# Selective scan, front work: VectorE empties the front's PSUM bank, input loads and silu move, three decay buffers

## What is computed

```python
xc   = silu(causal_conv(x_in, conv_w, 4 taps) + conv_b)          # [2, 2048, 512]
proj = xc @ xp_w.T                                               # 64 + 16 + 16 columns
dt, Bm, Cm = split(proj, [64, 80])
dt   = softplus(dt @ dt_w.T + dt_b)                              # [2, 2048, 512]
A    = -exp(A_log)                                               # [512, 16]
def step(h, (x_t, dt_t, B_t, C_t)):
    dA = exp(dt_t[:, :, None] * A)
    h  = dA * h + (dt_t * x_t)[:, :, None] * B_t[:, None, :]     # state: 512 channels x 16
    y  = einsum('bdn,bn->bd', h, C_t) + D * x_t
```

## Time and profile before

| | us |
|---|---|
| median of 3 runs | 4641.67 (4637.85 to 4651.1) |
| the profiled execution, its own time | 4628.16 |
| its span | 4626.6 |
| first scan to last scan | 251.8 to 2048 |
| mean length of a unit (15 from silu to silu) | 112.6 |
| busy in 256 to 1945: PE / DVE / ACT / POOL | 1303.4 / 1310.8 / 1481.8 / 1321.6 of 1689 |

### The profile page before, as it was taken

How to read it: one execution, slowest core, us unless ns; L and a number is a source line. 1 busy time by engine, 2 the same in 40 slices (tenths; PEclk the granted TensorE clock), 3 DMA queues, 4 the chain that set the end, 5 groups by cost and what they waited for, 6 DMA issues and landing times. The chain is left out here.

```text
span 4626.6 us, 69508 instructions
## 1 busy us (share of the span) xinstructions
PE 3557.3 (77%) x20742; PEld 2201.9 (48%) x20742; DVE 2819.4 (61%) x4258; ACT 2720.9 (59%) x4311; POOL 1749.6 (38%) x1132
## 2 busy tenths in 40 slices
PE   8477777777777777756775888888988885499990
PEld 4156666666666666645553222222222223366660
DVE  4267777777777777756675666666666665411105
ACT  3288888888888888864563455555555551011120
POOL 0067777777777777764342000000000002300006
PEclk9688889998888888877886899999999997699995
DMA  6443322233333333334545000100010103311115
GB/s 209 120 110 83 83 83 83 83 96 87 88 88 84 83 86 89 83 105 147 208 155 163 17 24 24 26 24 20 24 26 24 26 17 117 122 64 67 69 40 185
DMA packets 183442, 385.72 MB, mean 83 GB/s; under 512 B 21763, under 2 KB 96630, under 8 KB 168624
## 3 DMA queue, kind: packets, MB, share of 16 engines
q1 hardware_dynamic: 129360, 285.61, 21.3%
q10 hardware_dynamic: 39760, 51.81, 3.3%
q0 software_dynamic: 13968, 43.97, 2.8%
HBM read 272.97 MB, written 110.91 MB: 83 GB/s over the span
## 5 line engine op out<-in xcount | busy, mean ns | idle before, releaser
L730 DVE TENSOR_TENSOR_SCAN scan_hh<-scan_dA,scan_state,scan_bx 128x512 f32<-128x512 f32 x1024 | 1247.9, 1265 | 413.6 <-PE scan_bx L816 351.6
L507 POOL TENSOR_TENSOR scan_hC<-scan_hh,scan_cbc 128x1024 f32<-128x1024 f32 x512 | 1207.7, 2370 | 237.4 <-DVE scan_hh L730 137.2
L1464 DVE TENSOR_REDUCE attend_mx<-attend_s 128x1 f32<-128x512 f32 (+1 forms) x1360 | 781.5, 608 | 342.9 <-PE attend_s L1594 226.0
L816 PE MATMUL scan_bx<-kept_ident,scan_dBxT 128*128 128x128 f32 x4096 | 692.8, 297 | 104.6 <-DVE scan_hh L730 55.1
L573 ACT ACTIVATE scan_dBxT<-scan_dtxT,scan_bt 128x512 f32<-128x512 f32 x1028 | 655.8, 712 | 97.8 <-PE scan_bx L816 97.7
L826 PE MATMUL scan_acc<-kept_ident,scan_hC 128*128 128x128 f32 x4128 | 671.8, 292 | 43.1 <-ACT scan_uu L582 41.8
L568 ACT ACTIVATE scan_dA<-scan_dt,scan_an 128x512 f32<-128x512 f32 x1028 | 665.7, 714 | 50.6 <-DVE scan_hh L730 50.6
L816 PEld LDWEIGHTS scan_bx<-kept_ident,scan_dBxT 128*128 128x128 f32 x4096 | 525.5, 154 | 297.4 <-DVE scan_hh L730 154.2
L1558 ACT ACTIVATE attend_full<-attend_s 128x1024 f32<-128x1024 f32 x384 | 392.0, 1025 | 332.1 <-PE attend_s L1621 328.1
L1594 PE MATMUL attend_s<-attend_kt,attend_qt 96*128 96x512 bf16 (+1 forms) x1360 | 481.4, 372 | 130.9 <-DVE attend_mx L1464 73.3
L826 PEld LDWEIGHTS scan_acc<-kept_ident,scan_hC 128*128 128x128 f32 x4128 | 538.8, 153 | 47.2 <-ACT scan_uu L582 45.5
(11 more groups left out here) (219 smaller groups left out, 4502.3 us busy)
## 6 DMA issues: line engine op xcount, KB each, us to landing
scan_xs<-scratch_xin SPq DMA_DIRECT2D x288, 256.0 KB, 7.7
scan_cbc<-scratch_crows SPq DMA_DIRECT2D x64, 1024.0 KB, 5.0
scratch_qk<-mix_heads ACTq DMA_DIRECT2D x64, 384.0 KB, 10.0
scratch_y<-scan_uu ACTq DMA_DIRECT2D x17, 1024.0 KB, 4.2
attend_qt<-scratch_qk SPq DMA_DIRECT2D x34, 384.0 KB, 3.7
attend_kt<-scratch_qk SPq DMA_DIRECT2D x34, 384.0 KB, 4.5
mix_yf<-scratch_y SPq DMA_DIRECT2D x10, 1024.0 KB, 8.3
mix_yb<-scratch_y SPq DMA_DIRECT2D x10, 1024.0 KB, 12.0
```

Of the source, the lines that this page charges most:

```text
L507: pool.tensor_tensor(hC[n % 2][:, ms, :], h[:, ms, :], rows.unsqueeze(1).broadcast_to([P, 2, C]), ALU.mult).then_inc(hc_ok, 1)
L730: dve.tensor_tensor_scan(hh[n % 2][:, m, r], dA[n % 2][:, m, r], bx[bank(j)][:, r], state[:, d, n, m:m + 1], ALU.mult, ALU.add).then_inc(h ...
L816: last = pe.transpose(bx[bank(j)][:, t * P:(t + 1) * P], dBxT[turned_slot(n)][:, t, m * P:(m + 1) * P], k["ident"][:, :])
L1464: dve.tensor_reduce(mx[:, t, c:c + 1], s1[v % 2][:, 0:w], AX_X, ALU.max).then_inc(s1_read, 1)
```

## The change

- `conv_out` and `turned_out` move from ACT to DVE: an add of the bias (tensor_scalar, bank to SBUF) and a plain copy (bank to SBUF). In DVE's order each stands right behind the scan at whose j PE wrote the piece.
- conv of unit f + 2 is at j = 29, 33, 38, 43 (was 30, 36, 41, 58). All four blocks are ahead of turned dt*x, which stays at 49, 51, 53, 55.
- `silu` of unit f + 2 is in ACT's `tail(12)` of unit f, where `silu` of unit f + 1 was in `tail(0)`. Ahead of the first unit, ACT now runs silu twice.
- SP issues conv blocks 2 and 3 ahead of the last C rows (steps 12 to 15).
- dA has three buffers, in the order of dBxT's (`turned_slot`): n mod 3, but 1 for n = 15. `decay` waits by `decay_free`: three scans-of-a-step back in the middle of a unit, two for n = 15 and n = 1.

```diff
-        dA = [s.sb(f"dA{i}", [P, DT, C]) for i in range(2)]
+        dA = [s.sb(f"dA{i}", [P, DT, C]) for i in range(3)]
...
-        FR_PROJ, FR_BT, FR_DT, FR_NEXT, FR_TURN, FR_LAST, FR_ALL = 0, 1, 2, 6, 9, 13, 14
+        FR_PROJ, FR_BT, FR_DT, FR_NEXT, FR_TURN, FR_ALL = 0, 1, 2, 6, 10, 14
...
-        AT_DT, AT_NEXT, AT_TURN, AT_LAST, AT_SKIP = (18, 21, 24, 27), (30, 36, 41), (49, 51, 53, 55), 58, (14, 16, 19, 22)
+        AT_DT, AT_NEXT, AT_TURN, AT_SKIP = (18, 21, 24, 27), (29, 33, 38, 43), (49, 51, 53, 55), (14, 16, 19, 22)
...
+        def decay_free(n):
+            back = 1
+            while turned_slot((n - back) % NS) != turned_slot(n):
+                back += 1
+            return (n - back) * DT + 1 + HELD_H
...
-                        for g in range(2, 4):
-                            load_c(f, d, g)
+                        load_c(f, d, 2)
                         for m in range(2, DT):
                             sp.wait_ge(fr_mm, first + FR_NEXT + m - 1)
                             hold(sp, k)
                             load_x(nb, nc_, d, m)
+                        load_c(f, d, 3)
...
             def decay(d, q, n, m):
-                act.wait_ge(h_ok, q * DT + m + 1)
-                act.activation(dA[n % 2][:, m, :], dt[d][:, m, :], ACT.Exp, scale=an[:, d, m, n:n + 1]
+                if not (isinstance(q, int) and q == 0):
+                    act.wait_ge(h_ok, (q - n) * DT + decay_free(n) + m)
+                act.activation(dA[turned_slot(n)][:, m, :], dt[d][:, m, :], ACT.Exp, scale=an[:, d, m, n:n + 1]
                                ).then_inc(da_ok, 1)
...
                 def tail(n):
-                    if n == 0:
-                        silu(o, g, first - 1)
...
+                    if n == 12:
+                        silu(d, f + 2, first + FR_NEXT + 3)
...
+            def conv_out(d, f, m, group):
+                if m == 0 and not (isinstance(f, int) and f < 2):
+                    dve.wait_ge(skip_ok, f - 1)
+                    dve.wait_ge(front_ok, f - 1)
+                dve.wait_ge(fr_mm, group + 1)
+                dve.tensor_scalar(xc[d][:, m, :], fr[:, :], cb[:, d, m:m + 1], None, ALU.add).then_inc(fr_out, 1)
...
+            def turned_out(d, j, group):
+                dve.wait_ge(fr_mm, group + 1)
+                dve.tensor_copy(dtxT[d][:, j, :], fr[:, :]).then_inc(fr_out, 1)
...
+                        if at in AT_NEXT:
+                            i = AT_NEXT.index(at)
+                            conv_out(d, f + 2, i, first + FR_NEXT + i)
+                        if at in AT_TURN:
+                            i = AT_TURN.index(at)
+                            turned_out(o, i, first + FR_TURN + i)
```

36 lines of the change are left out of this document (8 added, 28 removed).

## The result

The changed kernel takes 4533.65 us (median, 4527.16 to 4550.5), the kernel before, on the same chip in the same rounds, 4646.39 (4637.85 to 4652.92). The ratio is 0.9764, with an interval of 0.9732 to 0.9796. The forecast was 4569, the range 4500 to 4632; "all early", one of the two ends of the forecast's own case, was 4537.

What follows compares the result with a forecast made beforehand. No engine full; waits, mostly scans for PE's bank, set a unit's length. Gains 5.1 + 0.6 - 1.5 = 4.2 (late) or 6.8 (early), at three to one 4.85, times 16, less 4.5 for silu ahead: 4569 us, range 4500 to 4632.

Steps and rivals of the forecast that it cites:

- all early: softplus_low on DVE starts ahead of POOL's product in every unit: gain 6.8 us a unit, 4537 us.
- Start of the unit: Scans 0 to 27: silu and conv_out of block 3 leave ACT's queue there, gain 5.1 us a unit.
- Scans 28 to 43: PE's conv waits go, DVE's waits for POOL come: gain 0.6 us a unit if softplus_low is late, 3.2 if early.
- all late: softplus_low on DVE comes behind POOL's product start and waits in every unit: gain 4.2 us a unit, 4579 us.
- Scans 44 to the next unit: DVE's four copies, handshakes of 0.4 and the boundary wait make this part 29.1 us, a loss of 1.5 a unit.
- silu's cover: ACT with silu at step 12 has step 14's first decay at t = 43, DVE needs it at 52: 9 us.
- place (c): PE's conv block 2 waits 5.70 us for its input, issued behind C rows that wait for POOL; forecast as gone.
- Meetings that cost nothing: Rival: POOL never mid-product when DVE's softplus_low, softplus, times_x come; 10.1 us a unit, 4485 us; chance 0.08.
- Dear handshakes: Rival: late everywhere, PE at half clock at scans 51, 53, 55, costing 3.6 us, not 0.4; 4630 us; chance 0.10.
- Copies that exclude POOL: Rival: DVE's copies behind scans 49, 51, 53, 55 wait for POOL, 1.9 us each; 4690 us; chance 0.05.
- silu that blocks step 14: Rival: silu on ACT delays scan 56 by up to 4.5 us, taking back the start's gain; 4640 us; chance 0.05.
- place (b): PE's conv block 1 waits 6.54 us for ACT to empty the bank, DVE then 3.95; forecast as gone.

Runs made afterwards that it cites:

- Experiment 7: Changed kernel with silu of unit f + 1 back in tail(0) and one silu ahead of the loop: 4605.3 us, ratio 0.9935.
- Experiment 1: Changed kernel with a DVE fill of 128 unused columns ahead of softplus_low in each unit: 4576.89 us, ratio 0.9853.
- Experiment 8: Changed kernel with the four copies of turned dt*x back on ACT: 4516.98 us, ratio 0.9751.
- Experiment 4: Changed kernel with two decay buffers instead of three, and the wait they need: 4529.48 us, ratio 0.9755.
- experiment 6: Changed kernel with the old load order, last C rows ahead of conv blocks 2 and 3: 4708.81 us, ratio 1.0161.
- experiment 2: Changed kernel with conv at j = 29, 33, 44, 46, so blocks 2 and 3 come behind times_x: 4520.63 us, ratio 0.974.

## Why the prediction was right, point by point

**Start of the unit.** 5.1 forecast, 5.3 measured. Experiment 7 shows its main term alone, 4.9 in these scans against 4.5. That ACT runs on without a gap from the boundary was the assumption under it, and it held up to the first piece of dt. Of the waits that I named as left, that before scan 12 was forecast at 2.5 and is 1.15, where before it was 2.76; those before scans 1, 2, 18 and 27 have grown by 1.1 together (18 from 1.41 to 1.91). In the sum they nearly cancel: ACT's queue is what binds this part, and where DVE stands for it is secondary.

**Scans 28 to 43.** The forecast's one miss is here, and only in the choice between its two cases. I worked out that softplus_low arrives at t = 12.18 and POOL is free at 12.10, and took the late side in three units of four, "since small delays can only push DVE to the late side". It arrives at 733.55 - 721.51 = 12.04 and POOL starts again at 733.57, t = 12.06. POOL's side was right to 0.04. DVE's was 0.14 too late, all of it in one term: scan 29 starts at t = 2.50 (724.01) and not at 2.64, the value that I took over from the scan behind conv in the earlier trace rows. There PE had waited 0.55 us for ACT; now it waits 0.17 and starts the conv at t = 0.81 and not 0.86. The other 0.09 lies between the conv and the scan. Timeline of PE:

```profile
722.32 1.06 PE L769 MATMUL scan_fr<-scan_xs,scan_taps 128*32 128x512 f32 x8 [0.17 <-ACT scan_ee L544]
```

The 7 scans and two conv_out behind it are 9.54 us, to the hundredth as forecast. And the units are no sample: softplus_low starts 12.04 us behind scan 28 in 12 of them and 12.09 in the other four, and in those four POOL is later by the same 0.05. Both engines' chains start from the same event, ACT's emptying of the last dt piece: in each unit ACT's exp starts 2.35 us behind that operation's end, and POOL's addition follows. A delay ahead of this event moves both, as in the four units; only one behind it can turn the order. So it was 16 of 16, and a share of three in four was never a likely outcome; the honest form was a chance for "all late" and one for "all early". That the 0.14 fell to the fast side was luck: nothing in the working could tell. Experiment 1 shows the other side, 4577 against 4579 worked out. Had I carried the two cases as such, the forecast would have been 4537 or 4579, with the measured 4533.65 at one of them. The terms as a whole hold: 6.8 a unit worked out for "early", 6.9 measured.

Behind that choice the working held: softplus and times_x wait 1.6 each (1.8 forecast), scan 44 starts at 32.6 behind the origin (754.07 - 721.51) where the early case gave 32.8, and the stretch gained 3.2.

**Scans 44 to the next unit.** A loss of 1.5 forecast, 1.7 measured. The copies are at a pitch of 0.58, 2.3 and not 2.4. The handshake's 0.4 came out by luck: DVE waits 0.34, but all of it before scan 49, where the piece stands ahead of the inject and no copy is waited for. At 51, 53 and 55, where the forecast had put it, PE waits 0.65 for each copy, and the scans run without a gap. The boundary is 2.6 for 2.5. What was missing is in the scans: two behind a copy take 2.55 and two behind a relu 2.44, so a pair between copies is 2.47 (762.09 to 764.56) and not 2.36, three times in a unit. Such a difference of 0.1 stood in no row of before. Experiment 8 says that ACT could have done the copies as cheaply.

**silu's cover.** On ACT the forecast held: silu done at t = 40 (761.71 is 40.2), the first decay of step 14 at 43 (764.18 and some 0.6 of it, 43.3). DVE was nearer: scan 56 starts at t = 49.7 and not 52, as it must where the early side has taken 2.6 us out of the unit. The cover is 6.4 us, not 9; enough. Timeline of ACT in after, the same unit:

```profile
757.19 1.28 ACT L524 ACT_TABLE_LOAD   x1
758.49 1.91 ACT L524 ACTIVATE scan_xc<-scan_xc 128x2048 f32<-128x2048 f32 x1
760.42 1.28 ACT L525 ACT_TABLE_LOAD   x1
761.71 2.56 ACT L568 ACTIVATE scan_dBxT<-scan_dtxT,scan_bt 128x512 f32<-128x512 f32 x4
764.18 2.54 ACT L563 ACTIVATE scan_dA<-scan_dt,scan_an 128x512 f32<-128x512 f32 x4
```

The two loads and silu are again 4.52 us from start to start (757.19 to 761.71). The Trainium skill's price for a switch ("ScalarE: Activation LUTs", What ACT_TABLE_LOAD costs) has its load of 1.28 in these rows and not its drain. By the page, two drains of 1.38 would make the move of silu worth 7.3 us a unit, an estimate; experiment 7 has 4.9 in scans 0 to 27 and 5.4 in all, and the measurement decides.

**The third buffer at nothing.** Experiment 4 agrees.

**The loads.** The forecast took place (c) as gone since the issue comes at t = 1.9. It comes at 2.1. Timeline of SP in after, to be held against the earlier trace rows:

```profile
723.65 6.55 SPq L436 DMA_DIRECT2D scan_xs<-scratch_xin  x8
738.06 0.35 SPq L445 DMA_DIRECT2D scan_cbc<-scratch_crows  x1
```

What I did not say is how much hung on it: experiment 6 shows 175 us or more.

**The rivals.** Meetings that cost nothing (4485) needed POOL never to be mid-product; it is, twice a unit. Dear handshakes (4630): none costs DVE over 0.44. Copies that exclude POOL (4690): 68 copies of 664 to 692 ns. All 64 in the loop overlap an operation of POOL that starts while the copy runs, and neither grows: the products there take 2.4 us, as ever. No copy started more than 0.07 us ahead of the end of a running operation, so that order isn't shown for copies; but 16 conv_out did start within POOL's addition, at 0.72 to 0.73 us. The Trainium skill's rule that the prediction drew on ("SBUF — State Buffer", the two separate sides) names only VectorE operations in a two-port mode or with two SBUF inputs, and these rows, which the trace of before lacked, agree for the copy and for conv_out. silu that blocks step 14 (4640): the cover held.

**What stays open.** The 10 us behind the scan stage; conv_out of blocks 0 and 1, whose move to DVE no experiment takes back alone (the trace shows only that place (b) is gone); the slower conv of experiment 1; and why in experiment 2 softplus took 3.7 us in 6 units and 2.27 in the others, where I know the meeting but not what set its phase from unit to unit.
